# First attention of a two-layer block: fewer products for mirrored blocks, whole-step VectorE instructions, and every weight's low part by accumulating DMA

## The reference, cut to what matters

```python
# 1: first attention, head_dim 8; here k = v = context, q = layernorm(x)
kv = einsum('bhil,bhjl->bijhl', k_, v_)              # products of all pairs of features
y = irfft(rfft(kv, n=2L) * rfft(ssm_kernel, n=2L))[..., :L]   # causal convolution along l
out = y + kv * D
out = einsum('bijhl,bhil->bjhl', out, q_)
# 2: mixture of experts: 16 experts of 128, 4 a token, and a shared one of 256
# 3: second attention (softmax over channels)
# 4: a feed-forward of 896 with 8 low-rank experts, 2 a token
```

## Time and profile before

| | us |
|---|---|
| median of 3 runs (lowest to highest) | 859.78 (859.76 to 860.88) |
| the profiled execution, its own time | 855.01 |
| its span (first to last instruction) | 853.3 |
| busy in the span: PE / DVE / ACT / POOL | 729.5 / 549.2 / 328.3 / 464.0 |

### The profile page before, as it was taken

One profiled execution on the slowest core, in us unless ns is written; L12 is line 12 of the kernel. 1 busy time (PEld: TensorE's weight loads), 2 busy tenths in 40 slices (PEclk: granted clock), 3 DMA queues, 4 the chain that ended last, 5 costly groups with the idle time before them and its releaser, 6 DMA issues.

```text
span 853.3 us, 14835 instructions
## 1 busy us (share of the span) xinstructions
PE 729.5 (85%) x5249; PEld 656.3 (77%) x5249; DVE 549.2 (64%) x1328; ACT 328.3 (38%) x680; POOL 464.0 (54%) x549
## 2 busy tenths in 40 slices
PE   4899989836778778238789999999999999999996
PEld 2344557736777778127789999999999999999996
DVE  4799977993445555348676767667666767654533
ACT  2221246612444445314454344444453343434321
POOL 4898963546455442336436636556475564543432
PEclk9899997967999999768899999999999999999999
DMA  8410014874555556342410201102011010000000
GB/s 257 152 38 12 26 37 122 186 157 160 147 152 144 139 146 123 106 139 77 127 35 25 65 1 57 32 13 63 13 32 57 1 50 27 1 14 1 2 13 13
DMA packets 42583, 63.16 MB, mean 74 GB/s; under 512 B 7152, under 2 KB 31760, under 8 KB 42512
## 3 DMA queue, kind: packets, MB, share of 16 engines
q1 hardware_dynamic: 34064, 38.71, 13.9%
q0 software_dynamic: 8352, 23.47, 12.3%
q10 hardware_dynamic: 96, 0.04, 0.0%
HBM read 47.37 MB, written 14.84 MB: 73 GB/s over the span
## 4 chain that ended last, share of the span: by engine, by line
PE 41%; DVE 6%; issue 4%; ACT 4%; POOL 3%; DMA 0%; POOLq 0%; ACTq 0%; DVEq 0%
PE bank L1387 15%; PE bank L1372 8%; PE bank L1419 6%; PE bank L1433 3%; PE bank L1405 3%; PE bank L1469 2%; DVE hid_lo L1883 2%; PE bank L1446 1%; ACT att_weights L1589 1%; POOL rows_back L1657 1%; DVE att_scaled L1793 1%; DVE am_lo L1872 1%; ACT am_hi L1574 1%; PE bank L1507 1%; ACT lora_w_hi L1550 1%
## 5 line engine op out<-in xcount | busy, mean ns | idle before, releaser
L1675 POOL TENSOR_TENSOR hid<-hid,rw_sb 128x256 f32<-128x256 f32 x112 | 90.7, 810 | 154.6 <-DVE hid L1877 154.4
L1387 PE MATMUL bank<-am_hi,lora_w_hi 128*128 128x256 f32 x448 | 126.9, 283 | 3.4 <-DVE am_lo L1872 3.4
L1877 DVE TENSOR_TENSOR hid<-hid,bank 128x256 f32<-128x256 f32 x112 | 46.7, 418 | 124.9 <-ACT hid L1557 124.2
L1387 PE MATMUL bank<-am_hi,lora_w_lo 128*128 128x256 f32 x448 | 126.7, 283 | 0.0
L1387 PE MATMUL bank<-am_lo,lora_w_hi 128*128 128x256 f32 x448 | 126.6, 283 | 0.0
L972 POOL DMA_INDIRECT rows_in<-y_scratch,slot_token x80 | 76.7, 958 | 76.5 <-DVE row_w L1173 44.6
L1557 ACT ACTIVATE hid<-bank 128x256 f32<-128x256 f32 x112 | 42.4, 385 | 183.3 <-PE bank L1387 170.7
L1387 PEld LDWEIGHTS bank<-am_hi,lora_w_hi 128*128 128x128 f32 x448 | 85.3, 190 | 3.6 <-POOL am_lo L1686 3.6
L1657 POOL DMA_INDIRECT rows_back<-slots_scratch,comb_idx x64 | 66.5, 1039 | 37.7 <-POOLq L666 22.2
L1387 PEld LDWEIGHTS bank<-am_hi,lora_w_lo 128*128 128x128 f32 x448 | 85.4, 191 | 0.0
L1387 PEld LDWEIGHTS bank<-am_lo,lora_w_hi 128*128 128x128 f32 x448 | 85.3, 190 | 0.0
(11 more groups left out here) (259 smaller groups left out, 2245.6 us busy)
## 6 DMA issues: line engine op xcount, KB each, us to landing
slots_scratch<-y_out SPq DMA_DIRECT2D x40, 256.0 KB
lora_stage_early<-in_lora_weights SPq DMA_DIRECT2D x16, 384.0 KB, 3.2
rows_in<-in_moe_weights SPq DMA_DIRECT2D x10, 384.0 KB, 3.9
moe_w_lo<-in_moe_weights POOLq DMA_DIRECT2D x10, 384.0 KB, 6.6
early_stage<-in_moe_weights SPq DMA_DIRECT2D x8, 384.0 KB, 7.5
x_sb<-in_x SPq DMA_DIRECT2D x4, 512.0 KB, 6.3
ctx_t<-in_ctx_t SPq DMA_DIRECT2D x4, 512.0 KB, 7.8
y_scratch<-y SPq DMA_DIRECT2D x8, 256.0 KB, 2.2
```

The source lines that it names most:

```text
L1387: last = nc.tensor.matmul(x_banks[F % 2][:, w * GT:(w + 1) * GT], wp, ap, start=False, stop=(half == 1 and k == 2), skip_group_check=True)
L1675: nc.gpsimd.tensor_tensor(f[:, F % 2, k, :], f[:, F % 2, k, :], rw_sb[:, F // FB % 2, k, :], ALU.mult)\
L1877: nc.vector.tensor_tensor(f[:, F % 2, k, :], f[:, F % 2, k, :], x_banks[F % 2][:, GT:2 * GT], ALU.mult)\
```

## The change

- **Mirrored blocks.** In odd steps POOL makes 48 products of 64 in two instructions (low by low 4 x 4, then all by high 8 x 4), PE's matmuls have 384 columns, and DVE reads the 4 x 4 block that is missing from its mirror: three multiplies (256, 256 and 512 elements) into one product tile. Even steps keep all 64.
- **Both halves in one instruction.** In even steps POOL's and DVE's multiply, and in all steps DVE's sum, take 1024 elements. There is one product tile: the sum waits for the multiply just ahead, and the next multiply for that sum.
- **Weights.** All 18 blocks are split in first_phase by high part, negative and accumulating DMA. The stage has two places, and a place is loaded anew once ACT has copied the high part. ACT does blocks 0 to 2 among the queries and blocks 3 to 17 in a row after the last query copy, ahead of all end_rows. POOL issues the DMAs at n = 5, 7, 9, 11, 12, 13, 14, 16, 17, 18, 19, 21, 22, 23, 24, 26, 27, 28. moe_phase has no weight work left.
- **Smaller moves.** ACT, not DVE, makes query rows 3. For the last four pairs DVE, not ACT, makes the high part (x_parts). x_t has three places. The last Toeplitz part is loaded ahead of the first weights. The tiles q_t, ctx_t, x_hi and x_lo are laid out by chunk. In moe_phase the order of the one-hot tables is 0, 1, 2, 3, with one wait earlier.

```diff
-STAGES, LATE_STAGES = 4, 2
+STAGES = 2
-LANE_ORDER = (0, 2, 1, 3)
+LANE_ORDER = (0, 1, 2, 3)
+LOWS_AT = {5 + 2 * k if k < 3 else 11 + 5 * (k - 3) // 4: k for k in range(FBLOCKS)}
+def distinct(n):
+    return n % 2 == 1
...
 # SP
-            for k in range(STAGES, SPLIT_EARLY):
-                sp.wait_ge(lo_split, k - STAGES + 1)
+            for k in range(STAGES, FBLOCKS):
+                sp.wait_ge(hi_split, 2 * (k - STAGES) + 1)
                 load_stage(k)
...
 # POOL
             def weights_low(k):
-                pool.wait_ge(hi_split, k + 1)
-                nc.gpsimd.tensor_tensor(w_lo[:, W_ORDER[k], :], stage[:, k % STAGES, :],
-                                        w_hi[:, W_ORDER[k], :].bitcast(FP32), ALU.subtract).then_inc(lo_split, 1)
+                pool.wait_ge(hi_split, 2 * k + 2)
+                nc.gpsimd.dma_start(w_lo[:, W_ORDER[k], :], a["moe_weights"][W_ORDER[k]], accum_op=ALU.add)\
+                  .then_inc(lo_split if k else first_low, 16)
...
-                if n % 4 == 2:
-                    weights_low(n // 4)
+                if n in LOWS_AT:
+                    weights_low(LOWS_AT[n])
...
+                feat = by_batch(ctx_t[:, c, :, :])[:, :, h * HEAD_DIM:(h + 1) * HEAD_DIM]
+                low, high = feat[:, :, 0:HALF_HEAD], feat[:, :, HALF_HEAD:HEAD_DIM]
+                for first, rows, columns in (((0, low, low), (OWN, feat, high)) if distinct(n) else ((0, feat, feat),)):
+                    shape = [P, HALVES * CHUNK_B, rows.shape[-1], columns.shape[-1]]
...
 # ACT
             def weights_high(k):
                 act.wait_ge(staged[k % STAGES], 16 * (k // STAGES + 1))
                 nc.scalar.copy(w_hi[:, W_ORDER[k], :], stage[:, k % STAGES, :]).then_inc(hi_split, 1)
+                act.wait_ge(hi_split, 2 * k + 1)
+                nc.scalar.mul(w_lo[:, W_ORDER[k], :], w_hi[:, W_ORDER[k], :].bitcast(FP32), -1.0).then_inc(hi_split, 1)
...
-            for p in range(FIRST_HALF):
+            query_copy(0)
+            query_rows(3)
+            for p in range(1, FIRST_HALF):
                 query_copy(p)
-            for k in range(STAGES):
-                weights_high(k)
-            weights_high(4)
+            weights_high(0)
+            weights_high(1)
             query_rows(4)
             query_rows(5)
+            weights_high(2)
             query_rows(6)
             query_copy(4)
             query_copy(5)
             query_rows(7)
-            weights_high(5)
             query_copy(6)
             query_copy(7)
-            weights_high(6)
-            weights_high(7)
+            for k in range(3, FBLOCKS):
+                weights_high(k)
             for e in range(FIRST_HALF):
                 end_rows(e)
                 x_columns(e)
+                x_high(e)
...
 # PE, conv(n)
-                    pe.wait_ge(prod_ready, HALVES * (n - CONV_SETS + 1))
+                    pe.wait_ge(prod_ready, n - CONV_SETS + 1)
+                cols = slice(0, KV_COLS if distinct(n) else ALL_COLS)
...
 # DVE, step n
+                if n >= 1:
+                    dve.wait_ge(reduced, n)
+                parts = ((everything, everything, out.rearrange("p n (j i) -> p n j i", i=HEAD_DIM)),)
+                if distinct(n):
+                    parts = ((low, low, out[:, :, 0:OWN].rearrange("p n (j i) -> p n j i", i=HALF_HEAD)),
+                             (low, high, out[:, :, OWN:2 * OWN].rearrange("p n (j i) -> p n j i", i=HALF_HEAD)),
+                             (high, everything, out[:, :, OWN:KV_COLS].rearrange("p n (i j) -> p n j i", j=HALF_HEAD)))
+                for j, i, y_ji in parts:
+                    shape = [P, width, j.stop - j.start, i.stop - i.start]
+                    last = nc.vector.tensor_tensor(prod[:, :, j, i], y_ji,
+                                                   query[:, :, i].unsqueeze(2).broadcast_to(shape), ALU.mult)
+                last.then_inc(prod_ready, 1)
                 if n in BACK_AT:
                     end_stats(BACK_AT[n])
+                dve.wait_ge(prod_ready, n + 1)
+                nc.vector.reduce_sum(query, prod[:, :, :, :], axis=AX.X).then_inc(reduced, 1)
...
-            pe.wait_ge(lo_split, 1)
+            pe.wait_ge(first_low, 16)
...
 # moe_phase
-                if q == 0:
-                    pe.wait_ge(lo_split, 16 * len(late))
-                for k in late_splits(m):
...
-            pool.wait_ge(hi_split, 2 * len(late))
-            dve.wait_ge(gu_done, SHARED_STEPS - 2 - SHARED_EARLY)
+            dve.wait_ge(gu_done, SHARED_STEPS // 2 - SHARED_EARLY)
```

More of the change, by code:

```diff
@@ L97, in build @@
     with ExitStack() as whole:
-        banks = [whole.enter_context(nc.psum_tensor(f"bank{i}", [P, 512], FP32)) for i in range(8)]
+        psum = whole.enter_context(nc.psum_tensor("psum", [P, 8, 512], FP32))
+        banks = [psum[:, i, :] for i in range(8)]
         def far(name, shape, dt=F32R):
@@ L403, in conv @@
                 if n >= CONV_SETS:
-                    pe.wait_ge(prod_ready, HALVES * (n - CONV_SETS + 1))
-                own, both = conv_banks[2 * banks_of:2 * banks_of + 2]
+                    pe.wait_ge(prod_ready, n - CONV_SETS + 1)
+                cols = slice(0, KV_COLS if distinct(n) else ALL_COLS)
+                own, both = (conv_out(n)[:, m * CHUNK_B:(m + 1) * CHUNK_B, cols] for m in range(HALVES))
+                first, second = (kv[:, slot, m * CHUNK_B:(m + 1) * CHUNK_B, cols] for m in range(HALVES))
                 same, across = toeplitz[:, h, 0:P], toeplitz[:, h, P:2 * P]
-                nc.tensor.matmul(own[:, :], same, kv[:, slot, 0, :], start=True, stop=True)
-                nc.tensor.matmul(both[:, :], across, kv[:, slot, 0, :], start=True, stop=False)
-                nc.tensor.matmul(both[:, :], same, kv[:, slot, 1, :], start=False, stop=True).then_inc(conv_done, 1)
+                nc.tensor.matmul(own, same, first, start=True, stop=True)
+                nc.tensor.matmul(both, across, first, start=True, stop=False)
+                nc.tensor.matmul(both, same, second, start=False, stop=True).then_inc(conv_done, 1)
             def attention_back(e):
@@ L526, in _ @@
             query_stats(1)
-            for p in range(FIRST_HALF):
+            for p in range(DVE_ROWS):
                 query_rows(p)
@@ L696, in hot_rows @@
             return v[:, rows, :].rearrange("p (t k) i -> p t k i", k=TOP_EXPERTS)
-        def late_splits(m):
-            return range(m * len(late) // SHARED_STEPS, (m + 1) * len(late) // SHARED_STEPS)
         STEPS_ROUTED = ROUTED_PAIRS + 4
@@ L959, in _ @@
                                         ALU.subtract).then_inc(lo_done, 1)
-                for k in late_splits(m):
-                    pool.wait_ge(hi_split, 2 * k + 2)
-                    nc.gpsimd.dma_start(w_lo[:, late[k], :], a["moe_weights"][late[k]], accum_op=ALU.add)\
-                      .then_inc(lo_split, 16)
             pool.wait_ge(table_ready, 1)
             pool.wait_ge(weights_stored, 16)
-            pool.wait_ge(hi_split, 2 * len(late))
             for i in range(ROUTED_TILES):
```

145 lines of the change are left out of this document (65 added, 80 removed).

## The result

The changed kernel took 868.90 us (median of 5 runs, 868.41 to 870.74), the kernel before on the same chip 860.88: ratio 1.0093, interval 1.0071 to 1.0115. It is slower, by 0.9%. I had forecast 854.1 us, with a range of 847.5 to 862. The profiled execution took 869.26 us, span 867.5, mean clock 0.939 (before: 855.01, 853.3 and 0.948).

A forecast was written before the change was run, and what follows sets the result against it. DVE's chain was to bound the steps: 17.5 + 82.9 + 9.0 + 1.5 + 2.8 = 113.7 us, 4.8 less; with 0.9 behind them, 5.7 less. Profiled 849.3, plus 4.8 to the median: 854.1 us, range 847.5 to 862.

The forecast's parts named there:

- DVE's chain: In the steps: each DVE instruction waits for the one ahead; even 2.52 us, odd 2.66, 32 steps 82.9 us.
- No hole at 21 us: Start of the steps: PE's 3.6 us hole behind n = 2 goes, and the slow clock behind it.
- The place of the wait: PE at the turn of rows 0, n = 22, waiting for ACT to end all 18 blocks; stall 2.8 us.
- the term for ACT and the loads: ACT's blocks 3 to 17: 2.1 us each up to block 8 at 52 us, then 3.0; rows at 81.8, stall 2.8.
- ACT is late at n = 22: slower: Rival at rows 0: loads every 3.9 us, block 17 starts 8 us later; 862, or 867 us; chance 0.16.
- the tail: Behind the steps: ACT loses four high copies of 0.62 us, DVE takes them; 0.9 us less (0 to 2.5).
- the tables: From 135 to 187 us: DVE is the limit with the same instructions, last two tables reordered; nothing counted.
- The first product: Start: query rows 3 made by ACT save 1.4 us (0 to 2.5), first product at 17.5 instead of 18.93.
- DVE's extras: Between the steps: DVE's query statistics and four times add, statistics and mean, together 9.0 us, counted whole.
- small waits: In the steps: waits between three close engines, and POOL's for ACT's first late block, 1.5 us (0 to 5).
- Kv products: POOL's products in the steps: 1.9 us for 1024 elements, odd step about 1.6, mean 1.75 against 2.01, 8 us less.
- The rival of the cheap chain: DVE's steps: a waited start costs no more than another, steps 75 us, end about 107; about 848 us; chance 0.20.

The follow-up runs named there:

- e10: Changed kernel with only accumulating DMAs moved: block 0's at step 5, blocks 1 to 14 at steps 18 to 31, last three after the products; 860.79 us, ratio 0.9997.
- e6: Changed kernel without the two stage places: each weight block loaded straight into its high part's tile, six loads ahead; 855.67 us, ratio 0.9974.
- e1: Changed kernel with rows 0 and 1 put between the weight blocks on ACT; 852.41 us, ratio 0.9927, and 0.9931 when measured again.
- e7: Changed kernel with rows 0 and 1 between blocks, no stage places, two product tiles, each sum behind the next step's multiply; ratio 0.9945.
- e5: Kernel before with POOL's low-part subtractions at n = 4, 8, ... 28 and 31 instead of 2, 6, ... 30; 853.13 us, ratio 0.9949.
- e2: Changed kernel without the 18 accumulating DMAs and the waits for them, so its output is not the reference's; 849.32 us in one run.

## Why the prediction was wrong

**Right.** DVE's chain: even steps 2.58 us (predicted 2.52), odd ones 2.72 (2.66). No hole at 21 us, full clock at the start. A small hole is left at 25 us, of the same kind: POOL waits 2.65 us for ACT's block 0 and PE idles for 1.71, but DVE does not. The place of the wait: PE at the turn of rows 0, n = 22, behind all 18 blocks on ACT. DVE would have come to product 22 at 82.4 (82.1).

**The step that failed** is the term for ACT and the loads: "I take that up to block 8, at 52 us. Then the accumulating DMAs run", and from there "4.9, a pace of 3.0 us". Block 3 was where I put it (43.1 against 42). But block 8 came at 58.5, because the accumulations crowd the loads from block 6 on, not from behind 8: POOL issued those of blocks 3, 4 and 5 at 45.1, 47.3 and 49.7 us, and ACT's copy of block 6 came 4.5 us after that of block 5. Without them e10 has block 8 at 53.7. Those are 6.5 us, 1.1 of them block 3's. The pace behind it was 3.3 instead of 3.0 us, 2.8 us more over nine blocks. Rows 0 were ready at 91.0, not 81.8. Then 2.3 us that I had not counted: the turn and most of the convolution behind the wait ran at a granted clock of 0.50, so that from the rows' end to the end of convolution 22 it was 5.4 instead of 3.1 us. Together 11.6; the stall was 14.15 instead of 2.8 us, 11.35 more, and with it the steps end at 124.9 instead of 113.7. It is the rival "ACT is late at n = 22: slower", to which I gave 0.16. Its time (862 to 867) assumed the pace from block 8 and a full clock. The miss adds up: the steps end 11.2 us late, the tail is 1.15 and the tables are 1.3 us worse than forecast, and the kernel before had 860.88 us beside it instead of 859.78: 854.1 + 11.2 + 1.15 + 1.3 + 1.1 = 868.9.

**Why it was mis-sized.** I had the engines' time right: 2.3 us for an accumulation, 1.2 us for a load, so 3.5 us of engine time for each block, against a step of 2.6 us. Four accumulations in five steps and as many loads need 4 x 3.5 = 14 us of 13: the engines were overbooked by my own figures. The late-ACT rival has half of that sum (29% of the engines left for loads, one every 3.9 us; 1.2 / 0.29 is 4.1), but my own term did not use it. I took the landing of the earlier trace rows instead, measured where ten blocks came within 33 us, 3.6 us apart (ACT's copies in the kernel before, 141.18 to 173.99 us), and stretched it by a guess. The measured pace lies between the two, since the accumulations lagged, as I had argued against the rival: from 40 to 75 us 9 of them were issued beside 11 loads. e6 shows that with the engines full 2.9 us a block is what one gets, while the landing grows to 13.8 us with the number of loads that are out.

**Smaller steps.** The first product came at 18.78, not 17.5: the turn of pair 3 ended 0.3 us before the old one, not 1.4. Convolution 0 took 3.8 us: its first matmul took 1.91 us, the length seen behind the wait at half clock, although the granted clock is 1.00 in the rows there; why is open. DVE's steps are 0.06 us longer than forecast, 1.3 us up to n = 22, since what waits for the sum starts 0.10 us after its end, not 0.04. Against that, DVE's extras cost 4.5, not 6.1 us up to there, and its small waits 0.9, not 1.5, which is why the arrival fits: that agreement is luck. So is the likeness of e1's end of the steps, 113.4 us, to my 113.7. e1 has no stall, and my sum without one is 110.9: e1 has 1.6 us more from the start, 1.9 from the chain and 1.8 from small waits (3.3 against 1.5), and 2.8 less from the extras. Kv products alone last 1.89 and 1.60 us, as predicted. The tail was to gain 0.9 us and lost 0.25. From 135 us on I counted nothing; 1.3 us were lost (last section). The rival of the cheap chain had a sum that does not come out: its own terms give 17.5 + 72 + 9 = 98.5 us for PE and 17.5 + 75 + 9 + 1.5 = 103 for DVE, not "about 107". And a pace of 4.4 us would have made the stall 15 us, not 16.

**The chain rival.** e7 is its test: a sum that waits for the multiply just ahead starts 0.03 us after its end (37.41 + 1.23 to 38.67 in the changed kernel), one that doesn't 0.08 us before it: 0.12 us, as I had put it. The Trainium skill ("VectorE: DVE Perf Modes", section "The DRAIN you can't avoid") has a measurement of eight copies in which a semaphore costs nothing extra; these rows do not agree with that as a rule. The same section says that a next instruction that is not held starts earlier, and with that they do. The gain of e7 did not reach the steps' end, so what the chain costs in this kernel's total is not shown.

## What to carry to other kernels

Add up the DMA engines' time of both directions of a pipeline (here 2.3 + 1.2 us a block) and hold it against the pace that it must keep, before believing a landing time that was measured at a slower pace. Where an engine has bulk work and a small result that three engines wait for, put the small result between the bulk: here that was the whole difference between 0.9% slower and 0.7% faster. And ask of each gain whether the old kernel could have it alone: one condition in the kernel before (e5) brought half a per cent.

## What the runs showed of the hardware

**An accumulating DMA held the engines for 2.2 us per 0.393 MB, a plain load for 1.2 us** (queue rows above; by the same rows 2.1 and 1.2 us in e6, and 1.4 for a load in e2). The Trainium skill ("DMA: Bandwidth & Descriptors", "Rules for kernel authors") says that an accumulate reads its destination and writes it later. It gives no price; more engine time than for a plain load fits that, and the rows have 1.8 times as much.

**Behind its wait PE went on at half its clock**: the granted clock was 0.50, the 1.2 GHz level, after 14 us of idling in the changed kernel and after 2.65 us in e10. Convolution 22 took 1.9 us more for it in the one and 1.1 in the other. After the 1.71 us of idling at 25 us the clock was still 1.00.

**DVE's small instructions are held by POOL's subtraction.** DVE and POOL of the changed kernel in order of time, behind the choice of experts:

```profile
163.32 1.26 DVE L1091 TENSOR_TENSOR tile_start<-tile_end,tiles_of 128x16 f32<-128x16 f32 x1
...
167.49 1.34 DVE L1104 TENSOR_SCALAR tile_at<-slot_best 128x128 f32<-128x128 f32 x1
```

```profile
163.26 1.29 POOL L974 TENSOR_TENSOR moe_act_lo<-moe_act,moe_act_hi 128x512 fp32r<-128x512 f32 x1 [6.14 <-ACT moe_act_hi L900]
167.46 1.29 POOL L974 TENSOR_TENSOR moe_act_lo<-moe_act,moe_act_hi 128x512 fp32r<-128x512 f32 x1 [2.90 <-ACT moe_act_hi L900]
```

In the kernel before, the same two are short. A subtraction begins beside the first, but 0.01 us behind it; the second meets none:

```profile
156.63 0.17 DVE L1080 TENSOR_TENSOR tile_start<-tile_end,tiles_of 128x16 f32<-128x16 f32 x1
...
159.71 0.23 DVE L1093 TENSOR_SCALAR tile_at<-slot_best 128x128 f32<-128x128 f32 x1
```

```profile
156.64 1.35 POOL L958 TENSOR_TENSOR moe_act_lo<-moe_act,moe_act_hi 128x512 fp32r<-128x512 f32 x1 [4.76 <-ACT moe_act_hi L878]
```

In the changed kernel the subtraction begins 0.03 to 0.06 us before each of the two, and each ends with it, some 1.1 us late. The Trainium skill ("SBUF — State Buffer", "Who interferes with whom") has it so: whoever issues first keeps the shared ports for its whole instruction, for a DVE instruction with two SBUF inputs or in a two-port mode; the rows agree. Which of them meet changes with every shift upstream. The stretch from the choice to the tables was 51.9 us before, 53.2 after, and 52.6 to 55.1 in e1, e2, e5 and e6. In the changed kernel the two cost 2.2 us, its four `tile_hot` products (L1116, mean 1.80 against 2.04 us) are 0.9 us shorter than before's, and 1.3 us are left. With such meetings a gain of 1 to 3 us ahead of this stretch can't be read from the total alone.
